# Expert tiles that claim two PSUM banks part by part, with biases added by a three-row bf16 matmul

## What is computed

```
x = x + rotary_attention(adaln_attention(x))
x = x + experts_0(quaternion_rotation(x))         # 8 experts, top 2, 128 -> 512 -> 128
u = experts_1(x)                                  # 8 experts, top 2, 128 -> 256 -> 256 -> 128
x = x + layernorm(log_linear_attention(u) + u)
x = x + ternary_ffn(adaln_attention(x))

experts_0: y_e = relu(x @ W1[e] + b1[e]) @ W2[e] + b2[e]
experts_1: y_e = relu(relu(x @ W1[e] + b1[e]) @ W2[e] + b2[e]) @ W3[e] + b3[e]
```

## Time and profile before

| | |
|---|---|
| median of 3 runs | 754.67 us |
| lowest, highest of them | 746.63, 755.76 us |
| profiled execution | 749.76 us, of which the span from the first to the last instruction is 747.9 us |
| busy share of the span | PE 66%, PEld 52%, DVE 54%, ACT 40%, POOL 33% |
| mean granted TensorE clock | 0.764 of full speed |

### The profile page before, as it was taken

The page is one execution under the profiler, slowest core; times in us unless marked ns, Lnnn a source line. Parts: engine busy times, 40 slices in busy tenths (PEclk is TensorE's granted clock), DMA queues, the critical chain, the costliest instruction groups (busy, mean ns, idle before and its releaser), DMA issues.

```text
span 747.9 us, 10481 instructions
## 1 busy us (share of the span) xinstructions
PE 494.3 (66%) x3533; PEld 387.7 (52%) x3533; DVE 400.3 (54%) x819; ACT 299.6 (40%) x837; POOL 249.9 (33%) x212
## 2 busy tenths in 40 slices
PE   2675857768588975467777677766777737766522
PEld 2464536556477864156666666544665526543311
DVE  1679989693866476500000100697626647856743
ACT  0243434434356653023323355332666634325421
POOL 1718573424813545530000400546230242425100
PEclk9787779976799998555555799786999959955555
DMA  9700000000244341134344567101345210000000
GB/s 323 213 16 0 1 1 1 1 1 15 65 133 117 104 128 29 49 96 108 108 118 126 156 190 194 31 1 47 107 123 140 65 36 4 1 1 4 1 4 7
DMA packets 79011, 53.54 MB, mean 72 GB/s; under 512 B 14608, under 2 KB 72912, under 8 KB 78704
## 3 DMA queue, kind: packets, MB, share of 16 engines
q1 hardware_dynamic: 76432, 48.37, 22.9%
q0 software_dynamic: 2048, 4.20, 1.9%
q10 hardware_dynamic: 480, 0.32, 0.2%
HBM read 44.34 MB, written 8.52 MB: 71 GB/s over the span
## 4 chain that ended last, share of the span: by engine, by line
PE 36%; DVE 29%; ACT 12%; issue 12%; POOL 4%; another core or an unknown queue 2%; DMA 1%; SPq 1%; DVEq 0%; POOLq 0%; ACTq 0%
PE PS L711 6%; PE PS L720 5%; DVE cond_ptbd L1131 3%; PE PS L694 3%; ACT hid L787 3%; DVE rot_qk L1312 3%; DVE rot_qk L1320 3%; POOL cond_kbd L981 2%; ACT hid L781 2%; PE PS L687 2%; DVE rot_ptbd L1340 2%; DVE rot_sh L1309 2%; DVE arena L1508 2%; PE PS L1207 2%
## 5 line engine op out<-in xcount | busy, mean ns | idle before, releaser
L1170 POOL TENSOR_TENSOR rot_sh<-rot_sh,const 128x1024 f32<-128x1024 f32 x16 | 49.3, 3091 | 55.2 <-DVE rot_sh L1309 55.2
L640 POOL DMA_INDIRECT picked<-slots_y,place_u x32 | 31.9, 995 | 104.7 <-DMA slots_y<-slot_y 96.3
L981 POOL TENSOR_TENSOR cond_kbd<-cond_qkv,const 128x2048 f32<-128x2048 f32 x16 | 58.5, 3654 | 21.3 <-ACT cond_qkv L1068 21.3
L720 PE MATMUL PS<-expert_w,hid 128*128 128x128 f32 x360 | 63.1, 321 | 2.6 <-ACT hid L787 2.0
L934 DVE SCALAR_TENSOR_TENSOR acc<-picked,weight,acc 128x128 f32<-128x128 f32 x8 | 2.8, 349 | 110.4 <-DMA picked<-slots_y,place_u 108.7
L711 PE MATMUL PS<-hid,expert_w 128*128 128x128 f32 x240 | 49.0, 368 | 19.4 <-ACT hid L781 19.3
L787 ACT ACTIVATE hid<-PS,expert_b 128x128 f32<-128x128 f32 x120 | 37.6, 365 | 48.4 <-PE PS L711 42.9
L720 PEld LDWEIGHTS PS<-expert_w,hid 128*128 128x128 f32 x360 | 54.7, 227 | 4.1 <-ACT hid L781 3.0
L711 PEld LDWEIGHTS PS<-hid,expert_w 128*128 128x128 f32 x240 | 42.2, 265 | 27.1 <-issue 26.9
L694 PE MATMUL PS<-slot_xT,expert_w 128*128 128x128 f32 x240 | 47.8, 334 | 2.4 <-ACT slot_xT L776 1.4
L781 ACT ACTIVATE hid<-PS,expert_b 128x128 f32<-128x128 f32 x120 | 37.6, 365 | 23.1 <-PE PS L694 20.9
(11 more groups left out here) (265 smaller groups left out, 1172.6 us busy)
## 6 DMA issues: line engine op xcount, KB each, us to landing
expert_w<-in_moe_w_dram SPq DMA_DIRECT2D x90, 256.0 KB, 3.0
expert_w<-in_moe_w_dram SPq DMA_DIRECT2D x60, 128.0 KB, 2.6
slot_x<-slots_x SPq DMA_DIRECT2D x60, 64.0 KB
slots_y<-slot_y SPq DMA_DIRECT2D x60, 64.0 KB, 2.3
slots_x<-zeros SPq DMA_DIRECT2D x2, 960.0 KB, 6.4
wqk<-in_attn_qk_dram SPq DMA_DIRECT2D x1, 1024.0 KB, 8.3
arena<-in_attn_qk_dram SPq DMA_DIRECT2D x1, 1024.0 KB, 8.8
expert_b<-in_moe_b_dram SPq DMA_DIRECT2D x60, 2.0 KB, 2.6
```

The costliest lines, as they stand in the source:

```text
L640: nc.gpsimd.indirect_dma_start(picked[:, j, n, :], None, ys[half], bass.IndirectOffsetOnAxis(place_u[job % 2][:, j, n:n + 1], 0)).then_inc ...
L720: mm = nc.tensor.matmul(full(MB_[i % 2], 0, E), hid[:, i % 2, c, :], W[i % WB][:, lo + E * (c - first):lo + E * (c - first) + E], start=(c ...
L981: nc.gpsimd.tensor_tensor(ckbd[:], cqkv[s][:, P:2 * P].unsqueeze(1).to_broadcast([P, CH, P]), k["headmask"].unsqueeze(2).to_broadcast([P, ...
L1170: nc.gpsimd.tensor_tensor(here, here, k["sin"].unsqueeze(1).to_broadcast([P, NC_ * SEQ, S]), ALU.mult).then_inc(rotated[part], 1)
```

## The change

- **Banks.** Both banks serve every tile. Bank 1 holds the transpose and hidden_a, bank 7 hidden_b and the output, in columns of their own. Each part claims its bank by itself: `transpose_slots(i)` now waits for `relu_a` of the tile before (and for `hidden_b(i-2)`, the last reader of its `slot_xT` buffer), hidden_a for the copy of the transpose, hidden_b for `copy_out(i-1)`, slots_out for `relu_b(i)`.
- **Biases.** A bias is split into three bf16 parts whose sum is the f32 value. Each of the four blocks of a tile begins with a matmul of these three rows with three rows of ones (bf16, `start=True`), onto which the f32 matmuls accumulate. The bias buffer is 3 partitions of 1 KB in place of 128 of 16 B.
- **ReLU.** One ACT instruction for 256 columns with no bias, in place of two for 128 columns with one.
- **Splitting.** In the first block SP loads the two bias tables (8 partitions of 2 KB each) after `wout`, and POOL makes the three parts, ten instructions on 8 partitions by 512 that wait for each other (six copies, four subtractions). In the second block SP first writes them to DRAM, and the first weight load waits for that.
- **Room.** `yq` and `yqT` of the last feed-forward move into a buffer that is free by then. `copy_u(0)`, `copy_feat(0)` and `places` get a wait each for buffers that are used twice.
- **Order.** The whole table `TIMES` is new. On PE, job 1 becomes a pattern over three tiles, in job 2 the transpose runs two tiles ahead:

The core of the diff, without the table:

```diff
-        MB_ = (1, 7)
+        MA_, MB_ = (1,) * 4, (7,) * 4
-        WBIAS = [sb(f"expert_b{n}", [P, FF0 // P]) for n in range(WB)]
+        WBIAS = [sb(f"expert_b{n}", [3, FF0], BF16) for n in range(WB)]
...
+        bias_in = [picked[0:EXPERTS, l].rearrange("e n f -> e (n f)") for l in range(2)]
+        bias_left = xT_half[0:EXPERTS, :].rearrange("e (c p) -> e c p", p=P)
+        bias_parts = [t.rearrange("e (s c p) -> e s c p", s=3, p=P) for t in (uT[0:EXPERTS, 0:3 * FF0 // 2].bitcast(BF16), acc[0:EXPERTS].rearrange("e n f -> e (n f)")[:, 0:3 * FF0 // 2].bitcast(BF16))]
+        bias_dram = [nc.dram_tensor(f"bias_parts{l}", (EXPERTS, 3, FF0), BF16, kind="Internal").ap() for l in range(2)]
...
+                for l in range(2):
+                    sp.dma_start(bias_in[l], d[f"moe{l}_b"].rearrange("e p c -> e (p c)")).then_inc(loaded["bias_in"], 16)
...
+                pool.wait_ge(loaded["bias_in"], 16 * 2)
+                own_split = Own()
+                for l in range(2):
+                    left = bias_in[l].rearrange("e (p c) -> e c p", c=FF0 // P)
+                    for part in range(3):
+                        nc.gpsimd.tensor_copy(bias_parts[l][:, part], left).then_inc(bias_split, 1)
+                        pool.wait_ge(bias_split, own_split.next())
+                        if part < 2:
+                            nc.gpsimd.tensor_tensor(bias_left, left, bias_parts[l][:, part], ALU.subtract).then_inc(bias_split, 1)
+                            pool.wait_ge(bias_split, own_split.next())
+                            left = bias_left
...
+                if i == 0:
+                    sp.wait_ge(bias_kept, 16 * 2)
...
-                sp.dma_start(WBIAS[i % WB][:], here("b").rearrange("o p c -> p (o c)")).then_inc(w_loaded[i % WB], 16)
+                kept = bias_dram[layer][s:s + 1] if s < EXPERTS else bias_dram[layer][bass.DynSlice(e, 1)]
+                sp.dma_start(WBIAS[i % WB][:], kept.rearrange("o s f -> s (o f)")).then_inc(w_loaded[i % WB], 16)
...
 
             def transpose_slots(i):
                 pe.wait_ge(x_loaded[i % XB], 16 * (i // XB + 1))
-                claim(pe, (MB_[i % 2],), (m_y_ready, i + 1))
-                nc.tensor.transpose(full(MB_[i % 2], 3 * P, 4 * P), slot_x[i % XB][:], k["ident"]).then_inc(m_xT_ps, 1)
+                if i >= 2:
+                    pe.wait_ge(m_b_ps, i - 1)
+                claim(pe, (MA_[job_of(i)[0]],), (m_xT_ready, i + 1))
+                nc.tensor.transpose(full(MA_[job_of(i)[0]], 3 * P, 4 * P), slot_x[i % XB][:], k["ident"]).then_inc(m_xT_ps, 1)
+
+            def add_bias(i, bank, at, f):
+                nc.tensor.matmul(full(bank, at, at + P), WBIAS[i % WB][:, P * f:P * f + P], ones_b[0:3, :], start=True, stop=False)
 
             def hidden_a(i):
                 job, half, layer, s = job_of(i)
                 pe.wait_ge(m_xT_ready, i + 1)
                 pe.wait_ge(w_loaded[i % WB], weights_up_to(i))
+                claim(pe, (MA_[job],), (m_a_ready, i + 1))
                 for f in range(2):
-                    mm = nc.tensor.matmul(full(MB_[i % 2], P * f, P * f + P), W[i % WB][:, P * f:P * f + P], slot_xT[i % 2][:], start=True, stop=True)
+                    add_bias(i, MA_[job], P * f, f)
+                    mm = nc.tensor.matmul(full(MA_[job], P * f, P * f + P), W[i % WB][:, P * f:P * f + P], slot_xT[i % 2][:], start=False, stop=True)
                 mm.then_inc(m_a_ps, 1)
 
             def hidden_b(i):
                 job, half, layer, s = job_of(i)
-                other = MB_[(i + 1) % 2]
                 pe.wait_ge(m_xT_ready, i + 1)
                 pe.wait_ge(w_loaded[i % WB], weights_up_to(i))
-                claim(pe, (other,), (m_b_ready, i + 1))
-                if layer == 0:
-                    for f in range(2, 4):
-                        mm = nc.tensor.matmul(full(other, P * f, P * f + P), W[i % WB][:, P * f:P * f + P], slot_xT[i % 2][:], start=True, stop=True)
-                else:
+                if layer:
                     pe.wait_ge(m_a_ready, i + 1)
-                    for f in range(2):
+                claim(pe, (MB_[job],), (m_b_ready, i + 1))
+                for f in range(2):
+                    add_bias(i, MB_[job], P * f, 2 + f)
+                    if layer == 0:
+                        mm = nc.tensor.matmul(full(MB_[job], P * f, P * f + P), W[i % WB][:, P * (2 + f):P * (3 + f)], slot_xT[i % 2][:], start=False, stop=True)
+                    else:
                         for c in range(2):
                             lo = FF1 + FF1 * c + P * f
-                            mm = nc.tensor.matmul(full(other, P * (2 + f), P * (2 + f) + P), W[i % WB][:, lo:lo + P], hid[:, i % 2, c, :], start=(c == 0), stop=(c == 1))
+                            mm = nc.tensor.matmul(full(MB_[job], P * f, P * f + P), W[i % WB][:, lo:lo + P], hid[:, i % 2, c, :], start=False, stop=(c == 1))
                 mm.then_inc(m_b_ps, 1)
 
             def slots_out(i):
                 job, half, layer, s = job_of(i)
                 pe.wait_ge(m_a_ready, i + 1)
                 pe.wait_ge(m_b_ready, i + 1)
+                claim(pe, (MB_[job],), (m_y_ready, i + 1))
                 first, lo = ((0, FF0), (2, 3 * FF1))[layer]
                 for c in range(first, 4):
-                    mm = nc.tensor.matmul(full(MB_[i % 2], 0, E), hid[:, i % 2, c, :], W[i % WB][:, lo + E * (c - first):lo + E * (c - first) + E], start=(c == first), stop=(c == 3))
+                    mm = nc.tensor.matmul(full(MB_[job], 2 * P, 3 * P), hid[:, i % 2, c, :], W[i % WB][:, lo + E * (c - first):lo + E * (c - first) + E], start=(c == first), stop=(c == 3))
                 mm.then_inc(m_out_ps, 1)
 
             def transpose_x(half):
...
 
             def copy_slots(i):
                 act.wait_ge(m_xT_ps, i + 1)
-                nc.scalar.activation(slot_xT[i % 2][:], full(MB_[i % 2], 3 * P, 4 * P), ACT.Copy).then_inc(m_xT_ready, 1)
+                nc.scalar.activation(slot_xT[i % 2][:], full(MA_[job_of(i)[0]], 3 * P, 4 * P), ACT.Copy).then_inc(m_xT_ready, 1)
 
             def relu_a(i):
                 act.wait_ge(m_a_ps, i + 1)
-                for c in range(2):
-                    ins = nc.scalar.activation(hid[:, i % 2, c, :], full(MB_[i % 2], P * c, P * c + P), ACT.Relu, bias=WBIAS[i % WB][:, c:c + 1])
-                ins.then_inc(m_a_ready, 1)
+                if i >= 2:
+                    act.wait_ge(m_out_ps, i - 1)
+                nc.scalar.activation(hid[:, i % 2, 0:2, :].rearrange("p c t -> p (c t)"), full(MA_[job_of(i)[0]], 0, 2 * P), ACT.Relu).then_inc(m_a_ready, 1)
 
             def relu_b(i):
                 act.wait_ge(m_b_ps, i + 1)
-                for c in range(2, 4):
-                    ins = nc.scalar.activation(hid[:, i % 2, c, :], full(MB_[(i + 1) % 2], P * c, P * c + P), ACT.Relu, bias=WBIAS[i % WB][:, c:c + 1])
-                ins.then_inc(m_b_ready, 1)
+                if i >= 2:
+                    act.wait_ge(m_out_ps, i - 1)
+                nc.scalar.activation(hid[:, i % 2, 2:4, :].rearrange("p c t -> p (c t)"), full(MB_[job_of(i)[0]], 0, 2 * P), ACT.Relu).then_inc(m_b_ready, 1)
 
             def copy_out(i):
                 act.wait_ge(m_out_ps, i + 1)
                 if i >= YB:
                     act.wait_ge(m_stored[i % YB], 16 * (i // YB))
-                nc.scalar.activation(slot_y[i % YB][:], full(MB_[i % 2], 0, E), ACT.Copy).then_inc(m_y_ready, 1)
+                nc.scalar.activation(slot_y[i % YB][:], full(MB_[job_of(i)[0]], 2 * P, 3 * P), ACT.Copy).then_inc(m_y_ready, 1)
 
             def copy_x(half):
                 act.wait_ge(routing, 4 * half + 1)
...
+                if half == 0:
+                    act.wait_ge(bias_kept, 16 * 2)
...
+                if job >= 2:
+                    dve.wait_ge(m_done, HT * (job - 1))
...
+                if n == 0:
+                    act.wait_ge(bias_kept, 16 * 2)
...
-        yq, yqT = fsb("yq", [P, HID], BF16), fsb("yqT", [P, NF, P], BF16)
+        yq, yqT = ffn_w[1][:, 0:HID // 2].bitcast(BF16), ffn_w[1][:, HID // 2:HID].bitcast(BF16).rearrange("p (f t) -> p f t", t=P)
...
+                for l in range(2):
+                    sp.dma_start(bias_dram[l], (uT[0:EXPERTS, 0:3 * FF0 // 2], acc[0:EXPERTS].rearrange("e n f -> e (n f)")[:, 0:3 * FF0 // 2])[l].bitcast(BF16).rearrange("e (s f) -> e s f", s=3)).then_inc(bias_kept, 16)
```

More of the change, by code:

```diff
@@ new lines @@
+    "m_transpose_u": (328.7, 483.3),
+    "m_gates": (358, 485.1),
+    "l_sum_gates": (362.1, 373.7, 375.6, 384.2, 489.2, 492, 500.1, 508.8),
+    "l_project": (330.6, 335, 371.8, 381.2, 486, 490.1, 501.1, 509.2),
+    "l_scores": (333.9, 370.9, 380.8, 402.3, 489.6, 499.2, 508.4, 521.8),
+    "l_times_u": (365, 377.1, 396.1, 403.8, 493.7, 504.7, 515.3, 529.7),
+    "l_output": (367.4, 379, 398.4, 407.9, 495.6, 506.6, 518.2, 532),
[6 rows of a table added]
+    "f_transpose_c": (405.7, 434.7, 461.2, 491.9, 529.1, 551.4, 572.4, 588.5),
@@ new lines @@
```

(17 more changed lines are left out.)

251 lines of the change are left out of this document (117 added, 134 removed), and 80 rows, old and new, of the table TIMES.

## The result

The change makes the kernel slower: 824.79 us in the median of four runs (814.47 to 827.24) against 752.95 us for the kernel before in the same comparison, a ratio of 1.088 with a 95% interval of 1.073 to 1.104. The ratio is taken from the runs of 814.47 and 822.54 us alone, as the other two (827.04 and 827.24) lie over 1.5% above the fastest and count as slow runs, so it is lower than that of the medians (1.095). The forecast was 704 us and faster. The profiled execution of the kernel after is its fastest one, 814.47 us, of which the span is 812.5 us; its mean granted clock was 0.744, that of the other three 0.712 to 0.724.

What follows compares the result with a forecast made beforehand. No engine is busy throughout, so the limit changes with the stage; job 1 is a chain of PE and ACT waits. From 749.8 us, -38 (job 1) -11 (job 2) +2 (job 0) -3 (job 3) +4 (start) gave 704, range 680 to 732.

Steps and rivals of the forecast that it cites:

- The price of the bias matmul: Each of 240 bias matmuls: 0.08 us at full clock, 0.16 at half, the next weight load overlapping; upper end 0.29.
- the other side: Rival, 3%: bias matmuls do not overlap, each stands for its full 0.314 us, 56 us come back: 760 us, slower.
- The clock: In job 1, PE waits only 0.8 of 14.5 us at half clock, so the clock rises after some three tiles.
- Job 1: Three tiles at half clock in 14.5 us, then 12 at 3.1 us: 52 us against 89.4, so -38.
- Job 2: Fifteen tiles of 2.8 us are 42, plus 3 us of waiting for a store: 45 against 56.3, so -11.
- Weights came late: Rival, 15%: in jobs 1 and 2 weight landing stretches to 4 us, tiles settle at about 3.4: 717 us.
- The new order gave not more: Rival, 8%: the new order gives 15 us more, in job 3 and the end of half 0: 689 us.
- a stall of 35 to 45 us: Rival, 9%: in jobs 0 or 3 an engine stalls because its new order doesn't fit real durations: 739 to 750 us.
- The clock at half in job 1: Rival, 15%: no rise in job 1, which takes 72.5 us (gain 17), and job 2 gains 6: 730 us.
- Start and the way to job 0: First block: POOL's ten splitting instructions make it ready at some 26 us in place of 22: +4 (ends 0 and +8).
- Jobs 0 and 3: Job 0: 4.8 us more PE time less shorter waits, +2 (-6 to +5); job 3: shorter ReLUs, -3 (-8 to +2).
- The ReLUs: On ACT, one 256-column ReLU without bias takes 0.384 us against 0.64 for the pair: each of 120 pairs shrinks by 0.25.

Runs made afterwards that it cites:

- rows128: The kernel after with bias matmuls of 128 rows (rows 3 to 127 zeros) in place of 3: 717.81 us, ratio 0.966 to the kernel before.
- bef3: The kernel before with a bf16 matmul of 3 rows of zeros added ahead of each of the 240 blocks: 855.3 us, ratio 1.149.
- r128_oldorder: rows128 with the table TIMES of the kernel before, so the old order on every engine: 724.35 us, ratio 0.961 to the kernel before.

## Why the prediction was wrong

**The price of the bias matmul** is the step that failed. "I take 0.08, because here too they stand in a stream in which the next load overlaps": it doesn't. 0.335 us at full clock and 0.505 at half stand in place of 0.08 and 0.16. The row it was taken from the earlier trace rows has 128 rows, and for 128 rows it was nearly right (0.10 and 0.20 in `rows128`). The upper end was wrong too: I took the duration of a single matmul, 0.314, for the most that one can cost. But a matmul that lets no load run ahead also lays bare the load of the matmul behind it, and that time stands in the f32 lines. And the rule from the Trainium skill (TensorE: Matmul & The Clock Gate, LDWEIGHTS), that the load costs its columns whatever the rows, answered another question: the load itself is as long (94 ns at 3 rows, 103 at 128), only it is no longer hidden. The rival "the other side" named the mechanism and had 3%. Its 760 us was short because it priced the matmuls at full clock and left the rise of the clock in jobs 1 and 2 standing.

**The clock.** I expected it to rise in job 1, since PE would wait only 0.8 of 14.5 us. It stayed at 0.50. With 128 rows in the same order it rose (0.86 over job 1), so the expectation held for the kernel I had in mind. What failed is that I took the idle time of PE in the profile as the sign of what the clock will do. Between two blocks of the kernel after the profile shows no idle time of PE, and still the clock stayed. Why is open. The runs show only that PE at 88% to 97% busy was left at half clock (`bef3` in job 2, the kernel after in job 1 and in most of job 2), and that in `r128_oldorder` the clock rose behind a tile with PE at 83% (4.97 of 6.00 us).

**Job 1**, -38. Given the right price my own count holds: 3 x (9 x 0.435 + 4 x 0.505) + 0.8 = 18.6 us for three tiles at half clock, measured 19.0 (18.7 in the first). With 128 rows the job took 57.8 us in place of 52. Its tiles at full clock take 3.2 to 3.6 us (344.5 to 354.1 to 364.2 to 375.0 for three each), not 3.1, the bias being 0.10 and some waits being left. But the larger part of the difference lies in the three tiles behind these, which take 16.2 us (375.0 to 391.2). PE stands 2.71 us before a hidden_a (376.31 to 379.02), and behind this wait the clock falls: it is 0.50 from 380.4 to 390.3.

**Job 2**, -11. The count gives 9 x 0.435 + 4 x 0.505 + 0.31 = 6.24 at half clock (measured 6.4), and at full 3.8 (measured 4.0): 88.1 us in place of 45. With 128 rows a tile takes 3.0, and the job 54.4, above all because the steps of the log-linear attention take 5.7 us between its tiles (4.6 of PE and a wait of 1.0). I had put these at nothing, since what they lengthen here they shorten behind: that was right, the stretch to job 3 is 7 us shorter. The wait of transpose_u(0) for the gathers, "1 or 2 us", is 1.02 in `rows128`.

**The other rivals.** Weights came late nowhere in the kernel after: the waits of PE in jobs 1 and 2 are for ACT but for one of 0.4 us, 9.9 us in sum. With 128 rows, where the tiles are nearly as short as forecast, 4.3 us of waits have no releaser in the trace; the rival supposed 12.6. The longest is the one of 2.71 us. It was for weights, by elimination: hidden_a waits for the copy of its transpose, for `relu_a` of the tile before and for its weights, the first two had ended by 375.3, and the last DMA of a weight load had been issued at 375.5. So this rival came true in a small way, and by the fall of the clock behind it cost more than the wait. The new order gave not more but nothing. No stretch shows a stall of 35 to 45 us; job 0 is the worst of jobs 0 and 3 with +9.7. The clock at half in job 1 came true, for a reason that the rival did not have.

**Start and the way to job 0.** POOL leaves the first block at 25.09 us, against 22.07, +3.0 where I had +4. The Trainium skill's figure for strided reads (GPSIMD Engine Reference, Performance pitfalls for Q7 kernels) gives an estimate of 1.7 us of that; the trace agrees: the first copy and subtraction of each table take 1.18 and 1.07 against 0.60, and 1.45 and 1.36 against 1.14, 1.6 us in sum. With these the ten instructions took 10.4 us (14.21 to 24.62), against 11.6 estimated without them. But I stopped there. From the first block to job 0 16.6 us more have been added, and `r128_oldorder` starts job 0 at 199.8 us where `rows128` does at 216.4, so it is the new order that adds them: one more tile of half 1's rotary attention stands ahead of the first slot tile. The prediction says nothing on it, though the diff of the table shows it.

**Jobs 0 and 3.** With 3 rows +9.7 and +1.1, forecast +2 and -3; with 128 rows -0.6 and -12.8. So what stands ahead of job 0 comes back in job 3 and before it, and the order as a whole changes nothing that can be told (`r128_oldorder`).

**The ReLUs** were 0.383 as taken from the earlier trace rows. Where the 0.25 us of each pair come from, the prediction did not say: most of it is the bias operand (365 ns against 274), not the pair. A pair without bias costs only 0.07 us more than the single instruction, 8 us for 120 pairs, and yet it cost 6 to 15 us in the new order and 18 to 28 in the old one (by the times and by the ratios), because there it goes with a clock that doesn't rise in job 1 (0.50 against 0.88).

The sum that full rows would have given is -32 us by the spans (747.9 and 715.6), as `rows128` has it, where I had -46; against the kernel before beside it, it is -24 (741.77 and 717.81).

## What to carry to other kernels

Before a matmul of few rows is put into a stream of full ones, look whether it has more than 64 rows; if not, fill its operands with zeros up to 128. The rows of zeros cost nothing that could be told here (96 rows and 128: 715.6 and 717.8 us), and between 64 and 96 nothing was run. Price an added matmul by the period from one block to the next in a kernel with the same shapes, not by its own duration, and if no row has its number of rows, give the case that it doesn't overlap real weight, once for each level of the clock. Where a stage may stand near the point at which the clock rises, run it with a repeated wait a little shorter or longer: here a shorter ReLU brought job 1 from 91.1 to 65.8 us, and a new order of everything brought nothing that could be told. Don't read from PE's busy share which way it will go.
